# Adding into y: two DMAs of 256 KB per state, or one of 512 KB

## The chip, the cores and the metric

The kernel runs on one core of one Trainium2 chip. The metric is device time in microseconds, from one launch to its end; lower is better.

## What is computed

Input is x, 16 batches of 512 tokens with 256 channels. Four blocks follow one another, each added to x after a layer norm:

```
x = x + attention(layernorm(x))     # 16 heads, causal, softmax
x = x + ffn(layernorm(x))           # base + shared + 2 of 6 routed low-rank experts
x = x + ssm(layernorm(x))           # the part that the change touches
x = x + ffn(layernorm(x))
```

The third block, cut to what matters:

```
xc    = silu(conv(x) + conv_b)                # causal, 4 taps
delta = softplus(xc @ Wd.T + bd)
B, C  = xc @ Wb.T, xc @ Wc.T                  # 16 numbers per token each
for every token t, every channel d, every state n < 16:
    h[d,n] = exp(A[d,n] * delta[d]) * h[d,n] + delta[d] * xc[d] * B[n]
    y[d]   = sum over n of h[d,n] * C[n]
out = (y * sigmoid(x @ Wg.T + bg)) @ Wo.T + bo
```

## The kernel before

Everything of one batch lies on chip. In the third block the 256 channels are C = 2 halves of 128 partitions, and the 512 tokens lie along the row, so that one tile is 128 x (2 x 512) f32. The 16 states (NS) are taken one after the other. For state n of batch s:

- GpSimd multiplies `u` (delta times xc) with the row of B, spread over the partitions, into `inp` (`inputs`, L1449); SP loads that spread row from memory (`load_b`, L872).
- ScalarE makes `dec` = exp(a_n * dt) (`decays`, L1032).
- VectorE runs the recurrence over the tokens as one scan into `hc` (`scan`, L1275). `hc` has three buffers (HC = 3).
- TensorE spreads the row of C into a bank (`spread_c`, L679), and VectorE multiplies `hc` by it in place (`product`, L1283). For n = 0 the product goes directly into `y`.
- For n = 1 to 15 of batches 0 to 13 GpSimd issues DMAs that add `hc` into `y` in SBUF (`add_state`, L1459, `accum_op=add`). The sum over the states is thus made by the DMA engines. In the last two batches (LATE) TensorE sums instead, and no such DMA is issued.

After the last state VectorE multiplies `y` with the gate (`gate_y`, L1290), TensorE projects it, and so on. A scan that writes buffer k % 3 of `hc` first waits until the product that was there has been added, and `gate_y` waits for the last add of its batch. An add waits for the one before it on the same bytes.

The four blocks of different batches run interleaved. Each engine walks through a common count of half units (`now`), 80 of them to a batch, and issues each piece when its number in a table (PE_AT, ACT_AT, DVE_AT, POOL_AT, SP_AT) is due. The tables fix the order on every engine, and semaphores fix the rest: an instruction that waits holds up all behind it on its engine. GpSimd's row has `inputs` and `add` in turns, with small pieces for the norms (`rsqrt`, L1420 to L1425) and experts (`weigh_low`, L1432) between.

SP's queue carries the other transfers: x in and out, the split q and k parts to memory (L838) and back in stacked form (`sq`, `sk`, L852), and the rows of B.

A `Tally` is a semaphore with its count: `at(turn, n)` is the value once n pieces of that turn are done, 16 for every DMA.

Of the kernel before, what the change touches and what calls it, by code (L numbers as in the profile page):

```python
# [7 lines left out]
ALU = mybir.AluOpType  # L8
# [48 lines left out]
def hybrid_block(nc, x, norm_w, wqk_t, bqk_c, wv_t, bv, wo_t, bo, conv_w, conv_b, wd_t, bd, wbc_t,  # L57
                 log_a, wg_t, bg, wso_t, bso, base_t, base_b, down_t, up_s, router_b, out):
    NB, T, D = x.shape
    C = D // P  # L60
# [3 lines left out]
    NS = log_a.shape[1]  # L64
# [15 lines left out]
    HC = 3  # L80
# [132 lines left out]
    with ctx:  # L213
        def sb(name, shape, dt=F32):
            return ctx.enter_context(nc.sbuf_tensor(name, shape, dt))

        def sem(name):
            return ctx.enter_context(nc.semaphore(name))

        def tally(name, per, step=1):  # L220
            return Tally(sem(name), per, step)
# [88 lines left out]
        y = sb("y", [P, 2, C, T])  # L310
# [4 lines left out]
        hc = sb("hc", [P, HC, C, T])  # L315
# [16 lines left out]
        def late_banks(s):  # L332
            return score_bank if s % 2 else max_bank
# [64 lines left out]
        inp_ready = tally("inputs", NS)  # L398
        scan_done = tally("scans", NS)
        hc_done = tally("products_with_c", NS)  # L400
        y_added = [tally(f"y_added{c}", NS - 1, 16) for c in range(C)]
        y_summed = tally("y_summed", NS)
        yg_done = tally("gated_y", 1)

# [720 lines left out]
        def _(dve):  # L1125
# [124 lines left out]
            def half_of_inputs(n):  # L1250

                if n == 0:
                    dve.wait_ge(u_done.sem, u_done.at(NB - 1))
                dve.wait_ge(b_ready.sem, b_ready.at(0, n + 1))
                V.tensor_tensor(inp[:, n % 2, 1, :], pv_bank[:, :], u[:, 1, :], ALU.mult).then_inc(b_used.sem, 1)

            def scan(s, n):
                k = NS * s + n
                old_s, old_n = divmod(k - HC, NS)
                if s == NB - 1 and n == 0:  # L1260
                    half_of_inputs(0)
                dve.wait_ge(dec_ready.sem, dec_ready.at(s, n + 1))
                dve.wait_ge(inp_ready.sem, inp_ready.at(s, n + 1))
                if s == NB - 1:
                    dve.wait_ge(b_used.sem, b_used.at(0, n + 1))
                if old_s >= LATE:
                    dve.wait_ge(y_summed.sem, y_summed.at(old_s - LATE, old_n + 1))
                elif old_n == 0:
                    dve.wait_ge(hc_done.sem, hc_done.at(old_s, 1))
                else:  # L1270
                    for c in range(C):
                        dve.wait_ge(y_added[c].sem, y_added[c].at(old_s, old_n))
                h, d, v = (t.rearrange("p c t -> p (c t)")
                           for t in (hc[:, k % HC, :, :], dec[:, n % 2, :, :], inp[:, n % 2, :, :]))
                V.tensor_tensor_scan(h, d, v, 0.0, ALU.mult, ALU.add).then_inc(scan_done.sem, 1)  # L1275
                if s == NB - 1 and n + 1 < NS:
                    half_of_inputs(n + 1)
# [7 lines left out]

            def gate_y(l):
                if l < LATE:
                    for c in range(C):
                        dve.wait_ge(y_added[c].sem, y_added[c].at(l))
                    V.scalar_tensor_tensor(y[:, l % 2, :, :], gate[:, l % 2, :, :], 1.0, y[:, l % 2, :, :], ALU.add,  # L1290
                                           ALU.mult).then_inc(yg_done.sem, 1)
                else:
                    dve.wait_ge(y_summed.sem, y_summed.at(l - LATE))
                    for c, m in enumerate(late_banks(l)):
                        last = V.scalar_tensor_tensor(y[:, l % 2, c, :], gate[:, l % 2, c, :], 1.0, m[:, :], ALU.add,
                                                      ALU.mult)
                    last.then_inc(yg_done.sem, 1)
# [39 lines left out]
            def side_work(now):  # L1337

                if (a := due(now, DVE_AT["gated"])) >= 0:
                    gate_y(a)  # L1340
# [45 lines left out]
            for now in range(START, STOP):  # L1386
                if now == -4 * HALF:
                    constants()
                unit, odd = divmod(now, 2)
                if not odd and 0 <= unit + LM < UN * NQ:  # L1390
                    maximum(unit + LM)
                if (g := group(now, DVE_AT["finish"])) >= 0:
                    finish_maxima(g)
                if (g := group(now, DVE_AT["heads"])) >= 0:
                    head_norm(g)
                side_work(now)
                for a, n in steps(now, DVE_AT["scan"]):
                    scan(a, n)
                for a, n in steps(now, DVE_AT["product"]):
                    product(a, n)  # L1400
# [3 lines left out]
        def _(pool):  # L1404
# [48 lines left out]

            def add_state(s, n):
                pool.wait_ge(hc_done.sem, hc_done.at(s, n + 1))
                for c in range(C):
                    if n > 1:
                        pool.wait_ge(y_added[c].sem, y_added[c].at(s, n - 1))
                    pool.dma_start(y[:, s % 2, c, :], hc[:, (NS * s + n) % HC, c, :],  # L1459
                                   accum_op=ALU.add).then_inc(y_added[c].sem, 16)  # L1460

            G.memset(ident[:, :], 0.0)
            G.memset(mask_qk[:, :], 0.0)
# [32 lines left out]
            for now in range(START, STOP):  # L1496
                if now == -4 * HALF:
                    behind()
                    G.memset(v_sb[:, :, :], 1.0).then_inc(pool_own.sem, 1)
                    pool.wait_ge(pool_own.sem, pool_own.one())  # L1500
                    G.memset(sk[KS:KS + 2, :, :, :], 1.0).then_inc(pool_own.sem, 1)
                    pool.wait_ge(pool_own.sem, pool_own.one())
                    G.memset(dec[:, :, :, 0:1], 0.0).then_inc(pool_fills, 1)
                    pool.wait_ge(pool_fills, 1)
                    pool.wait_ge(dve_const, 1)
                side_work(now)
                for a, n in steps(now, POOL_AT["inputs"]):
                    inputs(a, n)
                for a, n in steps(now, POOL_AT["add"]):
                    if n and a < LATE:  # L1510
                        add_state(a, n)
# [36 lines left out]
```

## Time and profile before

| | |
|---|---|
| three runs | 1925.6, 1930.14, 1930.07 us; median 1930.07 |
| the profiled execution's own time | 1925.6 us |
| its span, first to last instruction | 1923.0 us |
| mean granted TensorE clock | 0.977 |
| TensorE / VectorE / ScalarE / GpSimd busy | 1713.8 / 1676.4 / 1400.5 / 1102.4 us |
| software queue (the adds) | 60480 packets, 110.13 MB |
| hardware queue (SP) | 155682 packets, 163.17 MB |

In the rows, PE is TensorE, PEld its weight loads, DVE VectorE, ACT ScalarE, POOL GpSimd and SP the sync engine. L1459 is line 1459 of the kernel. "y<-hc" is an instruction that reads `hc` and writes `y`. Times in a window count from the start of the span. An idle time is put down to what ended it; "issue" is idle time for which the profile names nothing.

### The profile page before, as it was taken

What the parts mean: (1) busy time and instruction counts of PE and PEld (TensorE: products, weight loads), DVE (VectorE), ACT (ScalarE), POOL (GpSimd) and SP (SyncE); (2) the same over time, 40 slices, a digit from 0 to 9 for tenths busy, and PEclk for the clock granted to TensorE, in tenths of its full rate; (3) what the DMA queues carried; (4) which work ended last, traced back from release to release, by engine and by line L of the source; (5) the groups of instructions that cost most, each with busy time, mean ns of one, the idle gap of its engine ahead of it and who ended that gap; (6) DMA issues with size and microseconds to landing.
All of it is one profiled execution on the core that took longest, in us unless ns stands there. A gap on an engine that the chain in (4) does not pass through costs nothing.

```text
span 1923.0 us, 31523 instructions
## 1 busy us (share of the span) xinstructions
PE 1713.8 (89%) x9575; PEld 1006.4 (52%) x9620; DVE 1676.4 (87%) x3928; ACT 1400.5 (73%) x2724; POOL 1102.4 (57%) x903
## 2 busy tenths in 40 slices
PE   6989797999989898999999898999999898878875
PEld 2555454646455564646465565646455464535333
DVE  4654889999999999999999999999999899977892
ACT  3666768787887978787887878787877868675541
POOL 2000575667666676657667666657667566666330
PEclk9999899999999999999999999999999999999997
DMA  5312576978879797988879797988889687661110
GB/s 142 90 56 78 127 170 138 182 157 178 154 158 182 159 181 150 183 156 179 157 164 178 158 185 151 180 155 179 152 169 170 150 169 147 137 127 49 56 60 11
DMA packets 216331, 275.30 MB, mean 143 GB/s; under 512 B 37170, under 2 KB 129123, under 8 KB 216163
## 3 DMA queue, kind: packets, MB, share of 16 engines
q0 software_dynamic: 60480, 110.13, 34.8%
q1 hardware_dynamic: 155682, 163.17, 33.4%
q8 instruction: 77, 1.26, 0.3%
q14 instruction: 92, 0.75, 0.1%
HBM read 128.49 MB, written 34.08 MB: 85 GB/s over the span
## 4 chain that ended last, share of the span: by engine, by line
PE 48%; DVE 15%; ACT 12%; issue 9%; DMA 8%; POOL 7%; SPq 1%; another core or an unknown queue 0%; POOLq 0%; DVEq 0%; ACTq 0%
PE bank L423 9%; DVE hc L1275 7%; PE bank L542 5%; PE bank L625 4%; DMA y<-hc 4%; PE bank L487 4%; PE bank L509 4%; PE bank L642 4%; POOL inp L1449 3%; PE bank L434 3%; DVE bank L1131 2%; PE bank L417 2%; ACT pt L916 2%; DVE hc L1283 2%; PE bank L626 2%
## 5 line engine op out<-in xcount | busy, mean ns | idle before, releaser
L1449 POOL TENSOR_TENSOR inp<-u,b_all 128x1024 f32<-128x1024 f32 x240 | 572.8, 2386 | 361.0 <-issue 125.0
L1275 DVE TENSOR_TENSOR_SCAN hc<-dec,inp 128x1024 f32<-128x1024 f32 x256 | 585.8, 2288 | 39.7 <-POOL inp L1449 15.2
L1131 DVE CUSTOM_DVE_ANT_0 bank<-bank,mask_qk 128x512 f32<-128x512 f32 (+3 forms) x1024 | 479.4, 509 | 85.6 <-PE bank L487 85.0
L1459 POOL DMA_DIRECT2D y<-hc x420 | 368.5, 949 | 129.5 <-DMA y<-hc 64.9
L916 ACT ACTIVATE pt<-bank 128x512 f32<-128x512 f32 x640 | 380.1, 605 | 72.5 <-PE bank L525 49.3
L1032 ACT ACTIVATE dec<-dt,a_neg 128x511 f32<-128x511 f32 x512 | 339.6, 729 | 34.1 <-DVE hc L1275 34.0
L1283 DVE TENSOR_TENSOR hc<-hc,bank 128x1024 f32<-128x1024 f32 x242 | 294.0, 1215 | 14.2 <-PE bank L679 13.3
L487 PE MATMUL bank<-sk,sq 96*128 96x512 bf16 (+3 forms) x1024 | 250.3, 306 | 27.3 <-DVE mall L1131 16.7
L509 PE MATMUL bank<-sq,sk 98*128 98x512 bf16 (+3 forms) x1024 | 248.6, 304 | 27.0 <-ACT pt L916 23.4
L542 PE MATMUL bank<-pt,v_sb 128*32 128x512 f32 (+3 forms) x2048 | 180.5, 450 | 7.5 <-ACT pt L916 6.8
L487 PEld LDWEIGHTS bank<-sk,sq 96*128 96x128 bf16 x1024 | 95.3, 99 | 145.0 <-issue 54.8
L949 ACT ACTIVATE parts<-bank,bqk 128x512 bf16<-128x512 f32 x192 | 131.3, 698 | 40.2 <-PE bank L423 24.1
L509 PEld LDWEIGHTS bank<-sq,sk 98*128 98x128 bf16 x1024 | 93.0, 99 | 117.7 <-ACT pt L916 47.9
L423 PE MATMUL bank<-xt_q,wqk 128*128 128x512 f32 x256 | 128.6, 627 | 18.1 <-ACT bcs L1012 16.1
L1131 DVE DVE_READ_ACCUMULATOR2_ANT mall<- 128x1 f32 x1024 | 144.4, 141 | 0.0
L679 PE MATMUL bank<-bcs,onehot 96*128 96x512 bf16 x256 | 98.9, 387 | 35.4 <-DVE hc L1283 21.2
L1423 POOL TENSOR_TENSOR rs<-va,half 128x4 f32<-128x4 f32 x64 | 71.5, 1117 | 87.2 <-DVE ng L1185 83.2
L642 PE MATMUL bank<-xs_t,taps 128*128 128x512 f32 x256 | 115.5, 594 | 0.2
L515 PE MATMUL bank<-mask_kq,ident_bf 128*128 128x256 bf16 x384 | 106.1, 276 | 0.0
L1198 DVE SCALAR_TENSOR_TENSOR X<-bank,X 128x256 f32<-128x256 f32 x192 | 73.3, 420 | 24.7 <-PE bank L434 13.9
L542 PEld LDWEIGHTS bank<-pt,v_sb 128*32 128x32 f32 x2048 | 48.1, 110 | 77.8 <-issue 58.0
L1432 POOL TENSOR_TENSOR hw<-low,wts 128x448 f32<-128x448 f32 x32 | 37.1, 1160 | 74.3 <-DVE wts L1232 74.1
(169 smaller groups left out, 2999.0 us busy)
## 6 DMA issues: line engine op xcount, KB each, us to landing
y<-hc POOLq DMA_DIRECT2D x420, 256.0 KB, 4.9
b_all<-b_kept SPq DMA_DIRECT2D x256, 256.0 KB, 3.7
qk_parts<-parts SPq DMA_DIRECT2D x96, 256.0 KB, 3.0
sq<-qk_parts SPq DMA_DIRECT2D x384, 64.0 KB, 3.7
sk<-qk_parts SPq DMA_DIRECT2D x384, 64.0 KB, 3.9
X<-in_x SPq DMA_DIRECT2D x16, 512.0 KB, 6.1
out<-X SPq DMA_DIRECT2D x16, 512.0 KB, 3.3
sq<-hlt SPq DMA_DIRECT2D x256, 2.0 KB
```

Of the source, the lines that this page charges most:

```text
L423: last = mm(dst[:, :], w[:, c, g * P:(g + 1) * P], src[:, c, :], start=(c == 0), stop=(c == C - 1))
L487: return mm(dst[:, o:o + n], sq[0:KS, slot, h, qb * P:(qb + 1) * P], sk[0:KS, slot, h, 0:n], start=True, stop=True)
L509: mm(dst[:, o:o + n], sk[:, slot, h, kb * P:(kb + 1) * P], sq[:, slot, h, kb * P:T], start=(o == 0), stop=True, skip_group_check=(o > 0))
L542: last = mm(pv_bank[VW * i:VW * (i + 1), kb * P:T], values_of(a, kb, first + i), pt[:, n % PT, at:at + T - kb * P], start=start, stop=stop ...
L642: last = mm(m.tile[:, :], taps[:, c, k, :], xs_t[:, c, k:k + T], start=(k == 0), stop=(k == TAPS - 1))
L916: A(pt[:, n % PT, :], score_bank[unit % 2][:, :], ACT.Exp).then_inc(exp_done.sem, 1)
L1032: last = A(dec[:, n % 2, c, 1:T], dt[:, c, 1:T], ACT.Exp, scale=a_neg[:, c, n:n + 1])
L1131: return V.tensor_tensor_reduce(src[:, o:o + n], src[:, o:o + n], mask_qk[:, T - n:T], 1.0, -3.0e38, ALU.add, ALU.max, out)
L1275: V.tensor_tensor_scan(h, d, v, 0.0, ALU.mult, ALU.add).then_inc(scan_done.sem, 1)
L1283: V.tensor_tensor(hc[:, k % HC, :, :] if n or s >= LATE else y[:, s % 2, :, :], hc[:, k % HC, :, :], spread_bank[:, None, :].to_broadcast( ...
L1449: G.tensor_tensor(inp[:, n % 2, :, :], u[:, :, :], b_all[:, k % 3, None, :].to_broadcast([P, C, T]), ALU.mult).then_inc(inp_ready.sem, 1)
L1459: pool.dma_start(y[:, s % 2, c, :], hc[:, (NS * s + n) % HC, c, :], accum_op=ALU.add).then_inc(y_added[c].sem, 16)
```

## The change

The two DMAs of a state, one for each half of the channels, become one over both halves, and the two semaphores with their waits become one.

```
-        y_added = [tally(f"y_added{c}", NS - 1, 16) for c in range(C)]
+        y_added = tally("y_added", NS - 1, 16)
...
                 else:
-                    for c in range(C):
-                        dve.wait_ge(y_added[c].sem, y_added[c].at(old_s, old_n))
+                    dve.wait_ge(y_added.sem, y_added.at(old_s, old_n))
...
             def gate_y(l):
                 if l < LATE:
-                    for c in range(C):
-                        dve.wait_ge(y_added[c].sem, y_added[c].at(l))
+                    dve.wait_ge(y_added.sem, y_added.at(l))
...
             def add_state(s, n):
                 pool.wait_ge(hc_done.sem, hc_done.at(s, n + 1))
-                for c in range(C):
-                    if n > 1:
-                        pool.wait_ge(y_added[c].sem, y_added[c].at(s, n - 1))
-                    pool.dma_start(y[:, s % 2, c, :], hc[:, (NS * s + n) % HC, c, :],
-                                   accum_op=ALU.add).then_inc(y_added[c].sem, 16)
+                if n > 1:
+                    pool.wait_ge(y_added.sem, y_added.at(s, n - 1))
+                pool.dma_start(y[:, s % 2, :, :], hc[:, (NS * s + n) % HC, :, :],
+                               accum_op=ALU.add).then_inc(y_added.sem, 16)
```

## Rows read from the trace of the kernel before

**Rows 1.** The page's first part: busy us, share of span, instructions of each engine.

```profile
PE 1713.8 (89%) x9575; PEld 1006.4 (52%) x9620; DVE 1676.4 (87%) x3928; ACT 1400.5 (73%) x2724; POOL 1102.4 (57%) x903
```

**Rows 2.** Busy time by stretch: PE, PEld, DVE, ACT, POOL; then clock, DMA share, GB/s.

```profile
300.00:700.00 400.00, 367.76 (x2189) 224.88 (x2202) 381.88 (x904) 317.77 (x629) 262.84 (x220) 1.00 0.82 166
...
1720.00:1923.00 203.00, 154.67 (x517) 87.35 (x517) 144.76 (x179) 85.22 (x168) 73.51 (x50) 0.90 0.14 45
```

**Rows 3.** Waits of VectorE, whole span: total us, times, longest.

```profile
DVE hc L1275 <- POOL inp L1449: 15.2, 7, 4.0
...
DVE hc L1275 <- issue: 10.5, 13, 2.3
...
DVE hc L1275 <- DMA y<-hc: 2.7, 5, 1.3
...
DVE y L1290 <- DMA y<-hc: 0.5, 1, 0.5
```

**Rows 4.** Waits of VectorE from 1720 us to the end.

```profile
DVE hc L1275 <- POOL inp L1449: 11.3, 5, 4.0
```

**Rows 5.** A quiet pair of adds: GpSimd's timeline, then landings of first and second.

```profile
1165.31 0.85 POOL L1459 DMA_DIRECT2D y<-hc  x1 [0.33 <-DMA y<-hc]
...
1172.95 1.76 POOL L1459 DMA_DIRECT2D y<-hc  x2
...
DMA to landing us min/median/max: 3.4/3.4/3.4
...
L1459 POOL DMA_DIRECT2D y<-hc x1: 1176/1176/1176, 1173.5 to 1173.5; - x1
...
DMA to landing us min/median/max: 4.3/4.3/4.3
```

**Rows 6.** The page: queues (packets, MB, share of 16 engines); issues (KB, us to landing).

```profile
q0 software_dynamic: 60480, 110.13, 34.8%
q1 hardware_dynamic: 155682, 163.17, 33.4%
...
y<-hc POOLq DMA_DIRECT2D x420, 256.0 KB, 4.9
b_all<-b_kept SPq DMA_DIRECT2D x256, 256.0 KB, 3.7
qk_parts<-parts SPq DMA_DIRECT2D x96, 256.0 KB, 3.0
...
X<-in_x SPq DMA_DIRECT2D x16, 512.0 KB, 6.1
out<-X SPq DMA_DIRECT2D x16, 512.0 KB, 3.3
```

**Rows 7.** A busy pair and the next: GpSimd's timeline, then the first pair's landings.

```profile
1146.57 1.86 POOL L1459 DMA_DIRECT2D y<-hc  x2 [0.44 <-issue]
...
1153.16 0.87 POOL L1459 DMA_DIRECT2D y<-hc  x1 [1.78 <-DMA y<-hc]
1154.96 0.86 POOL L1459 DMA_DIRECT2D y<-hc  x1 [0.93 <-DMA y<-hc]
...
DMA to landing us min/median/max: 6.1/6.1/6.1
...
DMA to landing us min/median/max: 7.1/7.1/7.1
```

**Rows 8.** GpSimd's timeline: the first add of the batch whose last is in rows 5.

```profile
1082.83 1.77 POOL L1459 DMA_DIRECT2D y<-hc  x2 [0.34 <-DVE hc L1283]
```

**Rows 9.** GpSimd's and VectorE's timelines: the last add of the batch before, the gated product.

```profile
1065.47 1.76 POOL L1459 DMA_DIRECT2D y<-hc  x2
...
1071.37 0.42 DVE L1169 TENSOR_TENSOR ao<-bank,rc 128x256 f32<-128x256 f32 x1
1071.71 1.22 DVE L1290 SCALAR_TENSOR_TENSOR y<-gate,y 128x1024 f32<-128x1024 f32 x1
```

**Rows 10.** Waits of TensorE, whole span.

```profile
PE bank L487 <- DMA sk<-qk_parts: 8.0, 7, 2.4
```

## Prediction

> **What bounds the kernel now.** I read the page's busy shares first. TensorE is busy 89% of the span, VectorE 87%, ScalarE 73%, GpSimd 57% [rows 1]. An average over warm-up, steady part and tail hides the bound, so the next view is the busy time by stretch. In the steady part VectorE works 381.88 of 400 us (95%) and TensorE 367.76 (92%), while GpSimd, which issues the transfers that this change touches, works 262.84 (66%); the 16 DMA engines are at 0.82 of their time [rows 2]. So the steady part is a loop of VectorE and TensorE with about 18 us of VectorE idle in 400; GpSimd has a third of its time to spare, the DMA engines less than a fifth.
>
> The next question is whether VectorE's little idle time has anything to do with the adds into y. The list of its waits says: before a scan it waited 15.2 us in all for GpSimd's product `inp`, 10.5 us for nothing that is named, and 2.7 us for an add into y; before the gated product (L1290) 0.5 us for such an add [rows 3]. Of the 15.2 us, 11.3 lie after 1720 us [rows 4], where the last two batches run, which have no such adds. What is left and can be laid to the adds or to the engine that issues them is 3.9 + 2.7 + 0.5 = 7.1 us, and with all of the unnamed 10.5 it would be 17.6 us, 0.9% of the run. That is the ceiling of what a cheaper add can give.
>
> **The change part by part.** It replaces 420 transfers of 256 KB by 210 of 512 KB. The bytes are the same.
>
> *Issue on GpSimd.* One issue takes about 0.87 us, half of the pair's 1.76 [rows 5]. Nothing here shows a 4 KB row per partition being issued. If its price goes with the number of partition rows (128 either way), 210 x 0.87 = 183 us of GpSimd's busy time go. If it goes with bytes or with 2 KB pieces, nothing goes, a merged issue being the 1.76 us of the pair. I take the first, since each half is a whole row of 512 numbers and the two halves of y and of hc are neighbours in memory. Either way this lies beside other work in the steady part [rows 2], and is worth at most the 3.9 us of waits for `inp` outside the tail. I take 1.5 us.
>
> *Waits.* VectorE drops one of two waits before 210 scans and before 14 gated products. The two halves are signalled within about 1.5 us of each other and VectorE waited for them 3.2 us in all [rows 3], so a check of a count that is already there is what goes. I cost it at nothing; it is hidden by the instruction that VectorE is still running.
>
> *Landing.* This is what decides. In a quiet stretch the first half, issued at 1172.95, lands 3.4 us later, and the second, issued at 1173.5, lands after 4.3 [rows 5]. The pair is thus complete 4.85 us after its first issue, and the second half comes 1.5 us behind the first. That is the transfer itself: a software-queue packet takes 34.8% x 16 x 1923 us / 60480 = 177 ns, and 8 data packets per engine make 1.4 us [rows 6]. The DMA engines are therefore already kept full across the pair, and one transfer of double size should land after 3.4 + 1.5 = 4.9 us, as the pair does now. From below: a store of 512 KB lands after 3.3 us and one of 256 KB after 3.0 [rows 6], so doubling might cost 0.3 us and the merged add land after 3.7. From above: loads go from 3.7 (256 KB) to 6.1 us (512 KB) [rows 6], which would give 3.4 + 2.4 = 5.8; a merged issue of 1.76 us ahead of the first packet leads to the same 5.8. I take 4.9, since its rows are accumulating adds and the others are plain copies.
>
> In a busy stretch the pair issued at 1146.57 and 1147.57 (the last 0.86 of its 1.86 us) lands after 6.1 and 7.1 us, so it is complete after 8.1 [rows 7]. The extra 3.3 us over the quiet pair are packets of SP's queue in between, 33.4% x 16 x 1923 / 155682 = 66 ns each on average [rows 6]. With half as many packets of its own the merged add is interrupted less often; I take a quarter off the extra, so 7.3 us.
>
> The Trainium skill, "DMA: Bandwidth & Descriptors", section "Queues, rings and completion order", has each DMA engine alternate between the queues at packet borders. By that rule the merged add would lose up to half of the 3.3 us, and SP's transfers would lose it instead. The rows of before give means for each queue, no interleaving, so they neither confirm nor refute it.
>
> *What the merge takes away.* Now the halves form two chains: the next first half starts when the old first half has landed (1153.16), the next second half when the old second half has (1154.96) [rows 7]. Merged, the next add starts at about 1154.9, with both halves, and it is complete a full landing later. In the quiet case that is 4.9 us after the last one instead of 4.3, 0.6 us later for each add that follows directly on another. How much room is there? The fifteen adds of one batch start from 1082.83 [rows 8] to 1172.95 [rows 5]: 14 steps in 90.1 us, 6.4 us each. A typical merged add needs the median landing of one half, 4.9 [rows 6], plus the 0.6 to 1.0 us by which the second half is issued later, so 5.7, and 0.25 us until the next issue (1147.57 + 7.1 = 1154.7, then 1154.96 [rows 7]): 5.95, under 6.4. A busy one (7.3 + 0.25) overruns by 1.15 us and is made good over the two or three that follow. What is late next, if it isn't made good, is the gated product: in the frame shown the last add is issued at 1065.47 and complete at about 1070.3, and L1290 starts at 1071.71 behind the head normalisation, so it has 1.4 us to spare [rows 9]. I charge 0.1 us per batch, 1.5 us in all. Its bounds are 0 and the price of rival (B).
>
> *Sum.* -1.5 (GpSimd earlier) - 2 (part of the 3.2 us of waits for adds and of the unnamed ones) + 1.5 (serial adds) = -2 us on the profiled execution's 1925.6 us: 1923.6. The median of the three runs shown is 1930.1, 4.5 us above it; so I expect 1928 as the median.
>
> **The rivals.**
> (A) Same, as above: GpSimd's time falls and nothing that sets the end moves.
> (B) Slower by the chain of adds. If the merged add lands 0.9 us later than the pair (the upper end above), a typical one needs 5.7 + 0.9 + 0.25 = 6.85 us in a step of 6.4. That is 0.45 x 15 = 6.8 us per batch. Two pauses take some of it up: the last add but one is issued at 1165.31 and with the median landing complete at 1170.2, 2.75 us before the last one's issue [rows 5], and the gated product has its 1.4 us. The remaining 6.8 - 2.75 - 1.4 = 2.65 us x 14 batches = 37 us fall on VectorE: 1928 + 37 = 1965. It decides from a typical landing of 6.4 - 0.25 = 6.15 us upward. For it speaks that GpSimd already waits for landings before a next issue [rows 7] and that the DMA engines are at 0.82 [rows 2]; against it that the quiet pair shows the engines filled without a gap [rows 5].
> (C) Slower by SP's transfers. While a merged add runs, an SP packet may stand behind one of some 350 instead of 177 ns. A q/k load is 64 KB, 4 packets of 1 KB per engine, so up to 4 x 0.177 = 0.7 us later if each waits so. TensorE waited 8.0 us for these, 7 times [rows 10]. With twice as many late ones, and each of the 14 later by 0.7 us, 9.8 us come on top: 1938. It decides from about nine late loads (6 us) upward. For it speaks that the DMA engines are at 0.82 [rows 2]; against it that only 7 of 768 loads are waited for now.
> (D) Faster. If the merged add lands after 3.7 us, every wait for an add goes, and GpSimd, 183 us lighter, is never late outside the tail: up to 17.6 us, with the unnamed waits. I price it at 14, most of that ceiling, from the median of 1930: 1916. For it speaks a cheap doubling of the stores [rows 6]. Against it, only 7.1 us of waits name these engines [rows 3]. By the Trainium skill, "DMA: Bandwidth & Descriptors", section "Anatomy of one DMA — SWDGE (gpsimd) path", the fixed part is about 2.0 us and the rest bytes / 436 GB/s: an estimate of 2.6 us for one half and 3.2 for the merged add, close to this rival; the trace has 3.4 for a lone half [rows 5], so it disagrees for accumulating adds.
> (E) The change does nothing to the transfers: both halves still go as 2 KB packets, and an issue costs 1.76 us. Then landing is the pair's or (B)'s; its chance is held in (A) and (B).
>
> **How the numbers follow.** (A) 0.45, (B) 0.22, (C) 0.11, (D) 0.22. A measurement of this kernel tells about 0.3% (5.8 us) from no change, as its own runs span 1925.6 to 1930.1. (D) is faster, (A) same, (B) and (C) slower: 0.22, 0.45, 0.33. The range takes in most of (D) at 1917 and (B) to its price, 1965; (A) alone would be 1922 to 1935.
>
> **What the profile after would show.** 210 issues of 512 KB; their length (0.87 or 1.76 us) settles the issue; 30240 packets on the software queue instead of 60480, with about the same share. The landing of one add: 4.9 us in quiet stretches, a median under 6.15. GpSimd at about 48% of the span (1102 - 183 us). VectorE's waits for adds still a few us, at L1290 under 3. If instead L1290 or the scan waits tens of us for the adds, (B) holds; if L487 waits 15 us or more for q/k loads, (C). I am wrong if 4 KB accumulating packets take clearly more than double 177 ns, or if the steady frames have hidden room that a lighter GpSimd sets free.

## The result, and the profile after

The changed kernel takes 1945.3 us (median of 4 runs, 1943.89 to 1952.47) against 1927.84 for the one before: ratio 1.0082, 95% interval 1.0054 to 1.0109. It is slower by 0.8%, 16 to 17 us. All 29 executions on record lie between 1935.28 and 1952.47 us, with the median at 1943.78. The stated range of 1917 to 1965 held it, but only because it reached up to rival (B); the likeliest case, no change, was wrong, and so was the sign of the sum of -2 us.

The page after, beside [rows 1] and [rows 6]: busy shares, the queues, the issues of DMAs (KB, us to landing), and the groups of the scan and of the add (busy us, mean ns, idle time just before and what ended most of it).

```profile
PE 1722.2 (89%) x9620; PEld 1005.9 (52%) x9620; DVE 1679.5 (86%) x3928; ACT 1401.2 (72%) x2724; POOL 931.0 (48%) x693
...
q1 hardware_dynamic: 155682, 163.17, 33.7%
q0 software_dynamic: 30240, 110.11, 31.2%
...
L1274 DVE TENSOR_TENSOR_SCAN hc<-dec,inp 128x1024 f32<-128x1024 f32 x256 | 586.8, 2292 | 51.9 <-POOL inp L1447 16.8
...
L1456 POOL DMA_DIRECT2D y<-hc x210 | 186.1, 886 | 339.2 <-DMA y<-hc 295.0
...
y<-hc POOLq DMA_DIRECT2D x210, 512.0 KB, 5.4
...
X<-in_x SPq DMA_DIRECT2D x16, 512.0 KB, 7.3
```

GpSimd lost 171 us of work and half of the software queue's packets are gone, as intended. VectorE does the same work (1679.5 against 1676.4 us) in a span that is 19 us longer. The mean granted TensorE clock is 0.976 against 0.977, so the clock does not explain it. The waits say where VectorE stands. The groups of the scan and of the add on the page of before:

```profile
L1275 DVE TENSOR_TENSOR_SCAN hc<-dec,inp 128x1024 f32<-128x1024 f32 x256 | 585.8, 2288 | 39.7 <-POOL inp L1449 15.2
L1459 POOL DMA_DIRECT2D y<-hc x420 | 368.5, 949 | 129.5 <-DMA y<-hc 64.9
```

The idle time before scans rose from 39.7 to 51.9 us, which is 12 of the 19 us, and that before the products in place (L1283, now L1282) from 14.2 to 17.5. GpSimd's waits for landings ahead of an add rose from 64.9 to 295.0 us. In the trace of the changed kernel's repeat (below) the scans have 46.6 us and the products 21.3: the sum is much the same (67.9 against 69.4), the split is not. The list of VectorE's waits after, beside [rows 3] (total us, times, longest); the last row is that for `dec` before, which [rows 3] lacks:

```profile
DVE hc L1274 <- POOL inp L1447: 16.8, 7, 4.1
...
DVE hc L1274 <- issue: 15.3, 20, 2.5
...
DVE hc L1274 <- ACT dec L1032: 11.9, 14, 1.9
...
DVE hc L1274 <- DMA y<-hc: 5.6, 4, 2.3
...
DVE y L1288 <- DMA y<-hc: 0.3, 1, 0.3
...
DVE hc L1275 <- ACT dec L1032: 8.3, 13, 1.7
```

The add itself is named for 5.9 us, against 3.2, and the gated product, at which I had looked for the loss, waits 0.3. The largest growth is in "issue" (10.5 to 15.3) and in `dec` (8.3 to 11.9). In the repeat's trace "issue" stands at 17.8 and `dec` at 6.5, so only "issue" repeats. The stretch around 790 us, the longest single loss of this trace, shows how little such a name may say. First GpSimd's timeline (start, us, line, [idle before, what ended it]):

```profile
782.66 0.93 POOL L1456 DMA_DIRECT2D y<-hc  x1 [1.39 <-DVE hc L1282]
785.23 2.36 POOL L1447 TENSOR_TENSOR inp<-u,b_all 128x1024 f32<-128x1024 f32 x1 [1.64 <-issue]
792.08 0.88 POOL L1456 DMA_DIRECT2D y<-hc  x1 [4.49 <-DMA y<-hc]
792.71 1.23 POOL L1430 TENSOR_TENSOR hw<-low,wts 128x448 f32<-128x448 f32 x1
797.17 0.88 POOL L1456 DMA_DIRECT2D y<-hc  x1 [3.23 <-DMA y<-hc]
797.78 2.66 POOL L1447 TENSOR_TENSOR inp<-u,b_all 128x1024 f32<-128x1024 f32 x1
```

Then VectorE's and ScalarE's timelines there:

```profile
800.53 2.29 DVE L1274 TENSOR_TENSOR_SCAN hc<-dec,inp 128x1024 f32<-128x1024 f32 x1 [1.93 <-ACT dec L1032]
...
798.23 1.32 ACT L1032 ACTIVATE dec<-dt,a_neg 128x511 f32<-128x511 f32 x2
```

And the chain of waits there, in order of time:

```profile
782.66 8.88 DMA y<-hc
...
791.58 0.48 issue
...
792.08 4.56 DMA y<-hc
...
796.67 0.48 issue
...
797.17 4.57 DMA y<-hc
```

Read together: the add issued at 782.66 falls into a busy stretch and lands after 8.88 us. The next may only be issued then, half a us later, and lands after 4.56; the one after it again. GpSimd waits 4.49 and 3.23 us in its queue, and behind the second wait stands the next `inp`. It ends at 797.78 + 2.66 = 800.44, and the scan starts at 800.53. `dec` had ended at 799.55, so what the profile names is not what the scan waited for. Ahead of this place the scans run 7.8 us behind those of before (792.76 against 784.99), behind it 10.7 (800.53 against 789.86). Before the change the same states went through quicker, since each half followed its own predecessor. GpSimd's timeline of before, with the landing of the first half issued at 780.04:

```profile
780.04 0.87 POOL L1459 DMA_DIRECT2D y<-hc  x1 [0.23 <-issue]
781.63 0.85 POOL L1459 DMA_DIRECT2D y<-hc  x1 [0.72 <-DMA y<-hc]
782.19 1.26 POOL L1432 TENSOR_TENSOR hw<-low,wts 128x448 f32<-128x448 f32 x1
783.89 0.87 POOL L1459 DMA_DIRECT2D y<-hc  x1 [0.43 <-DVE hc L1283]
785.16 0.85 POOL L1459 DMA_DIRECT2D y<-hc  x1 [0.41 <-DMA y<-hc]
...
DMA to landing us min/median/max: 3.3/3.3/3.3
```

There the step from add to add is 3.85 us (780.04 to 783.89) and 3.5 for the second halves. The first of these was ended by the product, not by the landing; the landing of 3.3 us and half a us behind it would allow 3.8. After the change the step is 4.56 + 0.53 = 5.09 us (792.08 to 797.17).

The chain of the whole trace also shows a second path, rival (C)'s. In batches 1 to 4 (counted from 0) no add stands in it, but four late k loads do; they land after 6.2 to 8.1 us, where the median of such loads is 3.8. Here is the last of them and what follows it on TensorE and VectorE:

```profile
706.31 8.12 DMA sk<-qk_parts
...
714.47 0.39 PE L487 MATMUL bank<-sk,sq 96*128 96x512 bf16 x1 [0.73 <-DMA sk<-qk_parts]
...
721.61 1.22 DVE L1282 TENSOR_TENSOR hc<-hc,bank 128x1024 f32<-128x1024 f32 x1 [1.35 <-PE bank L679]
```

TensorE is late with the k rows, then with the row of C, and the product waits for it. From the first scan of batch 1 to that of batch 5 this took 434.25 us against 432.52 before: 1.7 us. From batch 1 to batch 14 the whole loss is 15.0 us (1418.81 against 1403.84), and behind batch 4 most of the chain's landings are adds. So the adds have the larger part of the loss and the late k loads a smaller one, whose size is not settled: with seven eighths of each add (below) two k loads of 8.4 and 8.1 us stand in the chain as well, and nothing is lost.

### The profile page after: what moved, and what is told of

It is laid out like the page before. It is cut to its first block, busy times and chain, and to the rows that moved or that the text cites. A ratio compares the mean times of both kernels' runs of the same rounds, so it can differ in the third digit from the quotient of the medians.

```text
span 1942.0 us, 31131 instructions
## 1 busy us (share of the span) xinstructions
PE 1722.2 (89%) x9620; PEld 1005.9 (52%) x9620; DVE 1679.5 (86%) x3928; ACT 1401.2 (72%) x2724; POOL 931.0 (48%) x693
## 3 DMA queue, kind: packets, MB, share of 16 engines
q0 software_dynamic: 30240, 110.11, 31.2%
## 4 chain that ended last, share of the span: by engine, by line
PE 39%; DVE 20%; ACT 12%; DMA 12%; issue 7%; POOL 6%; SPq 3%; POOLq 0%; DVEq 0%; ACTq 0%
DVE hc L1274 8%; PE bank L423 7%; DMA y<-hc 7%; PE bank L542 4%; DVE bank L1131 4%; PE bank L642 3%; DMA sk<-qk_parts 3%; PE bank L487 3%; PE bank L509 3%; SPq L852 3%; PE bank L434 3%; PE bank L625 2%; DVE hc L1282 2%; PE bank L417 2%; POOL inp L1447 2%
## 5 line engine op out<-in xcount | busy, mean ns | idle before, releaser
L1274 DVE TENSOR_TENSOR_SCAN hc<-dec,inp 128x1024 f32<-128x1024 f32 x256 | 586.8, 2292 | 51.9 <-POOL inp L1447 16.8
L1456 POOL DMA_DIRECT2D y<-hc x210 | 186.1, 886 | 339.2 <-DMA y<-hc 295.0
L1282 DVE TENSOR_TENSOR hc<-hc,bank 128x1024 f32<-128x1024 f32 x242 | 294.1, 1215 | 17.5 <-PE bank L679 16.5
L487 PE MATMUL bank<-sk,sq 96*128 96x512 bf16 (+3 forms) x1024 | 249.9, 305 | 34.0 <-DVE mall L1131 19.8
L487 PEld LDWEIGHTS bank<-sk,sq 96*128 96x128 bf16 x1024 | 94.6, 99 | 158.7 <-issue 58.3
L423 PEld LDWEIGHTS bank<-xt_q,wqk 128*128 128x128 f32 x256 | 47.0, 198 | 61.9 <-issue 58.4
```

The costliest lines, as they stand in the source:

```text
L423: last = mm(dst[:, :], w[:, c, g * P:(g + 1) * P], src[:, c, :], start=(c == 0), stop=(c == C - 1))
L487: return mm(dst[:, o:o + n], sq[0:KS, slot, h, qb * P:(qb + 1) * P], sk[0:KS, slot, h, 0:n], start=True, stop=True)
L1282: V.tensor_tensor(hc[:, k % HC, :, :] if n or s >= LATE else y[:, s % 2, :, :], hc[:, k % HC, :, :], spread_bank[:, None, :].to_broadcast( ...
L1456: pool.dma_start(y[:, s % 2, :, :], hc[:, (NS * s + n) % HC, :, :], accum_op=ALU.add).then_inc(y_added.sem, 16)
```

## Experiments

Two theories went in. S (serial): an add starts only when the whole one before has landed, GpSimd stands in that wait, and `inp` stands behind it. P (packets): the 4 KB packets of the software queue hold up SP's transfers. All times are medians, ratios are to runs of the kernel before on the same chip.

**The changed kernel again.** 

> The changed kernel again, as the base for the three others. Both theories: 1944 to 1947 us, ratio to before 1.008. Theory S (serial): an add may start only when the whole one before it has landed, GpSimd stands in that wait with the next product inp queued behind it, and the scan gets its inp late. Theory P (packets): packets of 4 KB on the software queue hold up the packets of SP's queue (rows of B, q and k parts), and those who wait for them lose the time.

Measured: 1946.15 us, ratio 1.0077 (1.0056 to 1.0098). The loss repeats, and so does its shape: 300.4 us of GpSimd's waits for landings, 17.8 us of "issue" before scans.

**Two DMAs as before, issued after a joint wait.**

```
             def add_state(s, n):
                 pool.wait_ge(hc_done.sem, hc_done.at(s, n + 1))
+                if n > 1:
+                    for c in range(C):
+                        pool.wait_ge(y_added[c].sem, y_added[c].at(s, n - 1))
                 for c in range(C):
-                    if n > 1:
-                        pool.wait_ge(y_added[c].sem, y_added[c].at(s, n - 1))
                     pool.dma_start(y[:, s % 2, c, :], ...)
```

> The kernel before, two DMAs of 256 KB with 2 KB packets and two semaphores, but GpSimd waits for both halves of the previous add before it issues either. S: as slow as the changed kernel or slower, since a pair lands 4.85 us after its first issue where the merged one needs 4.5: 1943 to 1965 us, ratio 1.008 to 1.02. P: packets are as before, so 1928 us, ratio 1.000.

Measured: 2013.53 us, ratio 1.0433 (1.0406 to 1.046). Packets, bytes and number of DMAs are those of the kernel before; only the wait is joint. It costs 84 us, five times the merge. So a joint wait is enough to lose time, and P, which said 1928, cannot give this. S stands, but its range was too low at the top. Whether the merge's own loss has this cause is what the run with every other add apart decides. The page's scan group and GpSimd's waits there:

```profile
L1275 DVE TENSOR_TENSOR_SCAN hc<-dec,inp 128x1024 f32<-128x1024 f32 x256 | 585.7, 2288 | 92.2 <-issue 55.8
...
POOL y L1460 <- DMA y<-hc: 363.1, 158, 6.0
```

**One DMA, meant to be cut into 2 KB pieces.** The edit is `max_dma_last_dim=T` in the DMA.

> The changed kernel, one DMA and one semaphore, but cut into pieces of 512 numbers (2 KB), 256 of them. S: not faster than the changed kernel, 1943 to 1965 us (the upper end if its issue takes 1.76 us on GpSimd). P: back to 1928 us. The landing tells what the packet size does to the add itself.

Measured: 2172.13 us, ratio 1.125 (1.1222 to 1.1278). The limit turned out to be in bytes: 218400 packets are 1040 for each add, so pieces of 512 bytes, and the run is not the one that I had meant. It still says something: issue and landing are the worst of all here, and so is the time.

```profile
L1456 POOL DMA_DIRECT2D y<-hc x210: 1537/1562/1737, 215.1 to 1957.2; - x105
...
DMA to landing us min/median/max: 6.4/6.6/11.9
```

**Every other add into a tile of its own.** The edit, cut to its core:

```
+                i = n % 2
+                if n > 2 or i:
+                    pool.wait_ge(y_added[i].sem, y_added[i].at(s, (n + 1) // 2 - 1))
+                pool.dma_start(y_odd[:, :, :] if i else y[:, s % 2, :, :], hc[...],
+                               accum_op=ALU.add).then_inc(y_added[i].sem, 16)
```

> The changed kernel, but the adds of odd states go into a tile of their own, each waiting only for the add two before it. The final sum of the two tiles is left out, and to make room two weight matrices of the same size share a tile with others, so that two loads are left out. Packets, bytes and issues are those of the changed kernel. S: GpSimd hardly waits for an add, the loss goes, 1915 to 1930 us, ratio 0.993 to 1.001. P: 1945 us, ratio 1.008.

Measured: 1927.75 us, ratio 0.9988 (0.9974 to 1.0001). The same 30240 packets, the same 210 issues, and the whole loss is gone once an add needn't wait for the one just before it. The two loads left out are not the reason: the control below leaves out the same two, and its ratio is 0.9994. The page's scan group is back at 37.6 us, though the adds themselves land later (median of both tiles 6.0 us), as they may now overlap:

```profile
L1274 DVE TENSOR_TENSOR_SCAN hc<-dec,inp 128x1024 f32<-128x1024 f32 x256 | 585.5, 2287 | 37.6 <-POOL inp L1448 16.8
...
DMA to landing us min/median/max: 4.5/6.0/9.9
```

This run also prices the gain that the merge was made for: with GpSimd some 170 us lighter and only 3.0 us of its idle time put down to a landing, the kernel is faster by 0.1%, about 2 us, if at all, since the interval reaches 1.0001.

**One DMA in pieces of 2048 bytes** (`max_dma_last_dim=4 * T`), the run meant above.

> One DMA and one semaphore as in the changed kernel, cut into pieces of 2048 bytes (in the run before, the limit of 512 turned out to be bytes: 1040 packets for each add). Theory S: what counts is the time from issue to landing of the whole add, plus about half a us until the next issue. If the pieces raise the issue from 0.88 to 1.0 to 1.76 us and the quiet landing from 4.5 to 4.9 to 5.7, the time lies between the changed kernel's 1946 and the 2013 of the pair with the joint wait, or up to 30 above that: 1950 to 2045 us. Theory P (4 KB packets hurt others): 1928 us.

Measured: 1984.97 us, ratio 1.0293 (1.0245 to 1.0341), inside S's range. Packets have their old size, and it is slower than with 4 KB. Issue and landing rose:

```profile
L1456 POOL DMA_DIRECT2D y<-hc x210: 1186/1202/1382, 214.3 to 1789.2; - x105
...
DMA to landing us min/median/max: 5.0/5.9/9.9
```

**Three quarters, and seven eighths, of each add.**

```
-                pool.dma_start(y[:, s % 2, :, :], hc[:, (NS * s + n) % HC, :, :],
+                to, add = (t.rearrange("p c t -> p (c t)")[:, 0:768]    # 896 in the other
+                           for t in (y[:, s % 2, :, :], hc[:, (NS * s + n) % HC, :, :]))
+                pool.dma_start(to, add,
                                accum_op=ALU.add).then_inc(y_added.sem, 16)
```

> The changed kernel, but each add covers only the first 768 of 1024 numbers of a row (3 KB packets); a quarter of y is left without its sums. The quiet landing should fall from 4.5 by a quarter of the 2.9 us of transfer, to 3.8. S: chain short enough, the loss goes: 1922 to 1931 us, ratio 0.997 to 1.001. If the loss came from the mere wait and order, not from its length: still 1940 or more.

> As the one with 768 numbers, with 896 (3.5 KB packets, an eighth of y left out). Quiet landing 4.15. S: part of the loss goes, 1928 to 1938 us, ratio 1.001 to 1.005.

Measured: 1924.57 us, ratio 0.9969 (0.9952 to 0.9985), and 1925.87 us, ratio 0.9979 (0.9961 to 0.9997). The second was a miss: I expected part of the loss to stay, and none did. The quiet landings are 3.9 and 4.2 us:

```profile
DMA to landing us min/median/max: 3.9/5.1/9.2
```

```profile
DMA to landing us min/median/max: 4.2/5.1/9.7
```

So 0.3 us less of landing take away some 20 us of time: there is an edge between 4.2 and 4.5 us. It does not lie in the mere amount of GpSimd's waiting. These are its waits for landings with 768 and with 896 numbers, against 64.9 us before and 295.0 merged:

```profile
POOL y L1458 <- DMA y<-hc: 106.2, 69, 5.3
...
POOL y L1458 <- DMA y<-hc: 184.7, 106, 4.6
```

With 184.7 us of such waits nothing is lost. One thing besides the length changed in both: they move fewer bytes (24.0% and 27.9% of the engines' time on the software queue instead of 31.2%), so the DMA engines are freer. The run with every other add apart lost nothing with all the bytes, so the bytes alone don't make the loss, but part of the step from 896 to 1024 may be theirs.

**Four buffers for hc, with the merged add and, as a control, with two adds.** The edit is `HC = 4`, with two weight matrices in shared tiles. The merged form was run twice.

> The changed kernel with four buffers for hc instead of three, so that a scan waits for the add four states back; two weight matrices share tiles with others and two loads are left out. S says that the loss falls on inp, which stands behind the waiting GpSimd, not on the scan's own wait for the add: 1940 to 1947 us, ratio 1.006 to 1.010. Rival H: the scan waits for the buffer, whatever the profile names: 1926 to 1934 us.

> The merged add with four buffers for hc once more, beside its own control, to settle what share of the loss is the scan's own wait for a buffer. If none: the ratio of this one to its control is 1.008, as with three buffers (1945 against 1928). If the third that the first run hinted at: 1.005 to 1.006.

> The control: the kernel before (two DMAs of 256 KB for each state) with four buffers for hc, the same two weight matrices sharing tiles and the same two loads left out. If buffers are no part of the matter, 1926 to 1930 us as before with three. If a fourth buffer helps whatever the adds are, 1920 to 1924 us, and then the gain seen with the merged add says nothing of the merge.

Measured: merged 1939.93 us, ratio 1.0058 (1.0034 to 1.0082), and in the repeat 1943.65, ratio 1.0069 (1.0049 to 1.009); two adds 1928.76, ratio 0.9994 (0.9982 to 1.0005). Merged against its control that is 1.0077, the same as with three buffers. So these runs can't tell that a scan's own wait for a buffer is any part of the loss; the first run's hint at a third did not repeat, though its interval overlaps the others. In these traces the idle time before scans is only 42.5 and 42.1 us merged, against 38.4 in the control. What grew more is the products' wait for the row of C, 20.2 and 21.0 against 13.7 us, and TensorE's waits for k rows are 14.1 and 15.2 against 9.0: the second path again.

**Side by side.** Quiet landing is the minimum from issue to landing; for the pair it is the 4.85 us of [rows 5], first issue to last landing.

| kernel | issue, us | quiet landing, us | idle before scans, us | time, us |
|---|---|---|---|---|
| before, each half after its own | 0.87 each | 3.2 each | 39.7 | 1928 |
| 768 of 1024 | 0.88 | 3.9 | 34.8 | 1924.6 |
| 896 of 1024 | 0.88 | 4.2 | 39.0 | 1925.9 |
| merged, every other apart | 0.88 | 4.5 | 37.6 | 1927.8 |
| merged | 0.88 | 4.5 | 51.9 | 1945.3 |
| merged, 2048 B pieces | 1.20 | 5.0 | 82.4 | 1985.0 |
| pair, joint wait | 1.76 for both | 4.85 | 92.2 | 2013.5 |
| merged, 512 B pieces | 1.56 | 6.4 | 170.3 | 2172.1 |

The time rises with the idle time before scans from the merged form on, but that time is not all of it: it covers 12 of 19 us of span there, and somewhat over half in the three slowest, where VectorE's own busy time rises too (1705.2, 1714.9 and 1757.0 against 1676.4 us). The idle time rises with the landing, with two exceptions. Every other add apart lands like the merged one and loses nothing, which is the point of that run. And the pair is slower than the 2048 B pieces though it lands sooner. It also holds GpSimd for longer, 1.76 against 1.20 us, before `inp` can start; that this explains the order is argued, not tested.

## Why the prediction was wrong, by its own steps

*Issue on GpSimd*: right. The issue takes 878 ns in the median for rows of 4 KB, about as for 2 KB (0.87 us), and GpSimd falls to 48%. Its worth, taken at 1.5 us, fits the run with every other add apart (about 2 us, not clear of zero).

*Waits*: the check that is gone was costed at nothing, and no run prices it. But the sum also took off 2 us for "part of the 3.2 us of waits for adds and of the unnamed ones", a term that no step had worked out. It went the other way: the waits for adds rose from 3.2 to 5.9 us and the unnamed ones before scans from 10.5 to 15.3.

*Landing*: right, on the safe side. I took 4.9 us in quiet stretches, measured were 4.5; the typical one was 5.4 against my 5.7. The upper end of 5.8 didn't come. (B) asked for a landing 0.9 us later than the pair's and a typical one of 6.15 or more; the merged add lands sooner than the pair, and the loss came all the same.

*What the merge takes away*: here it failed, in three places. The first is the comparison of a typical landing plus 0.25 us with the mean step of 6.4 us, 5.95 against 6.4. The steps aren't even. Where scans follow closely, `inp` waits for a scan and the next scan for `inp`. GpSimd's timeline of before shows that loop at its own pace:

```profile
1075.26 2.36 POOL L1449 TENSOR_TENSOR inp<-u,b_all 128x1024 f32<-128x1024 f32 x1 [3.60 <-DVE hc L1275]
1080.13 2.36 POOL L1449 TENSOR_TENSOR inp<-u,b_all 128x1024 f32<-128x1024 f32 x1 [2.51 <-DVE hc L1275]
```

From one to the next it is 4.87 us: a scan of 2.29 us, an `inp` of 2.36 us and 0.2 us between them, for the code lets `inp` of a state start only when the scan before it is done. An add needs landing plus half a us: 3.8 us by halves before, 4.4 with three quarters, 4.7 with seven eighths, 5.1 merged, 5.5 in 2048 B pieces. The edge in the experiments lies between 4.7 and 5.1, where this loop's 4.87 lies. As long as adds are quicker than the loop, a late one is made good behind it; once they are slower, it isn't until the tables leave a gap. This agreement is one of numbers; no run changed the loop's own length. A quiet step of 5.1 us overruns 4.87 by little, too: in the stretch around 790 us it was an add that landed after 8.88 us that began the loss, and the steps of 5.1 behind it that kept it.

The second is "the cost of an add that follows directly on another", 0.6 us. I compared landings and left out that two chains of halves each start when their own half is in: a step of 3.85 us became 5.09, so 1.2 us. The wait until the next issue was also half a us (791.54 to 792.08), where I took 0.25 from one row.

The third is "what is late next". I named the gated product and its 1.4 us. It waited 0.3 us in all. What stands directly behind the waiting GpSimd is `inp`, and behind `inp` the scan. I had that order in the code and checked only the two who wait for the add by semaphore. All three went into one term, the charge of 1.5 us for serial adds, and this is the step of the sum that failed. Measured, the loss is 16 to 17 us with the gain of a lighter GpSimd already in it, so what serial adds bring about, the late k loads included, is some 18 us.

*The rivals*: (B) had the place right (GpSimd waits for landings, the adds don't keep up) and the wrong victim, deciding point and price (37 us). (C), SP's transfers, had part of the path right and the cause wrong. L487's wait for k rows rose from 8.0 us in 7 waits to 12.7 in 14, and to 14.8, 14.1 and 15.2 us in the three other traces of merged adds, about at its sign of 15; x loads landed after 7.3 instead of 6.1 us. Some of this reaches VectorE, as the stretch at 706 us shows. But the 4 KB packets by themselves are not the reason. With every other add apart, at the same packets, the waits are 6.4 us in 6 and x loads land after 5.3 us; with 2048 B pieces the x loads stay at 7.2. Why k loads come late with merged serial adds is open. TensorE's list of waits after, and with every other add apart:

```profile
PE bank L487 <- DMA sk<-qk_parts: 12.7, 14, 2.4
```

```profile
PE bank L487 <- DMA sk<-qk_parts: 6.4, 6, 2.5
```

(D), faster by 14 us, had no room: the run with every other add apart gains about 2 us, if anything. (E) is refuted by the 30240 packets. As to the alternation of queues that the Trainium skill states ("DMA: Bandwidth & Descriptors", "Queues, rings and completion order"), no run here shows it or speaks against it.

## What to carry to other kernels

When a change joins two chains of dependent work into one, compare the latency of one link, with its reaction time, to the shortest loop beside it, not to the mean step. (Here 5.1 against 4.87 us says "slower" where 5.95 against 6.4 said "same"; that the loop sets the edge is not shown.) Then read the waiting engine's queue: the victim of an in-order engine's wait is whatever stands next in its queue, and the profile may name that wait "issue" or after another operand. Busy time freed on an engine with a third of its time idle was worth 0.1% at the median, not clear of nothing; the latency added to its waits cost 0.8%.

## What the runs showed of the hardware that I had not expected

- Adding 4 KB per partition in one piece is cheaper than twice 2 KB: a packet takes 31.2% x 16 x 1942 us / 30240 = 320 ns against 2 x 177, and the quiet landing is 4.5 us for 512 KB against 4.85 for the pair. Both packet times are means over all packets of the queue, of which an add has 144 for its 128 rows.
- The issue on GpSimd went with the number of pieces, not with bytes: 0.88 us for the 144 packets of one add with rows of 4, 3.5 or 3 KB (0.87 with 2 KB), 1.20 for 272, 1.56 for 1040.
- From a landing to the issue that waited for it half a us passed (791.54 to 792.08).
